# Gated cross-attention and top-2 expert block, 1 core: routed-row stores of the last two chunks placed one per expert tile

## What is computed

```python
x = x + tanh(g_xattn) * attention(layernorm(x), ctx, ctx)     # rotary q, k; 16 heads
n = layernorm(x)
xn = rms_norm(n) * norm_scale
scores = xn @ w_router.T                                     # 8 experts
ids = top_k(scores, 2); c = softmax(scores)[ids]
h = xn @ w_up[e].T; val, gate = split(h); h = val * silu(gate)
y = h @ w_down[e].T                                          # experts in ids only
x = x + tanh(g_ffn) * (sum(y * c) + n)
```

## Time and profile before

| | |
|---|---|
| median of 3 runs | 470.53 us (468.91 to 471.07) |
| the profiled execution | 470.41 us, of which 468.6 us is the span of the trace |
| PE busy | 411.8 us, 88% |
| DVE, ACT, POOL busy | 301.8, 261.7, 242.7 us |
| granted TensorE clock, mean | 0.917 of full |
| result stores (line 509) | 72, mean 1564 ns of POOL |
| row stores (line 427) | 64, mean 979 ns of POOL |

### The profile page before, as it was taken

How to read it: one execution, slowest core, us unless ns; L and a number is a source line. 1 busy time by engine, 2 the same in 40 slices (tenths; PEclk the granted TensorE clock), 3 DMA queues, 4 the chain that set the end, 5 groups by cost and what they waited for, 6 DMA issues and landing times.

```text
span 468.6 us, 13323 instructions
## 1 busy us (share of the span) xinstructions
PE 411.8 (88%) x3821; PEld 278.8 (59%) x3824; DVE 301.8 (64%) x1167; ACT 261.7 (56%) x582; POOL 242.7 (52%) x201
## 2 busy tenths in 40 slices
PE   7988899988898898989898939996799998999991
PEld 3445465645555466555555627674577876777871
DVE  6877888987878677777884414563655554555550
ACT  3437586977777676666665415752255554555540
POOL 6090242365446454454333475568466537886663
PEclk9998999999998897996956778998899999999997
DMA  7714341446579224232011322444334423344330
GB/s 185 177 47 126 75 112 35 121 135 173 145 206 232 63 65 115 77 88 79 30 43 48 87 52 43 68 59 94 59 48 61 58 47 49 56 57 56 37 28 0
DMA packets 57422, 39.07 MB, mean 83 GB/s; under 512 B 8819, under 2 KB 55158, under 8 KB 57366
## 3 DMA queue, kind: packets, MB, share of 16 engines
q1 hardware_dynamic: 43622, 28.87, 23.9%
q0 software_dynamic: 12736, 8.64, 13.1%
q10 hardware_dynamic: 1008, 0.85, 0.8%
HBM read 14.26 MB, written 11.75 MB: 56 GB/s over the span
## 4 chain that ended last, share of the span: by engine, by line
PE 61%; DVE 15%; issue 7%; ACT 5%; DMA 5%; another core or an unknown queue 4%; POOLq 1%; POOL 0%; DVEq 0%; ACTq 0%
PE bank L1595 9%; PE bank L1573 8%; PE bank L1575 7%; PE bank L1361 5%; DVE nmx L840 5%; PE bank L1585 4%; DMA out<-ys,yi 4%; PE bank L1388 3%; PE bank L1393 3%; PE bank L1335 3%; PE bank L1348 2%; PE bank L1303 2%; ACT pt L573 2%; PE bank L1304 2%
## 5 line engine op out<-in xcount | busy, mean ns | idle before, releaser
L509 POOL DMA_INDIRECT out<-ys,yi x72 | 112.6, 1564 | 63.8 <-issue 35.3
L427 POOL DMA_INDIRECT slots_dram<-xr,slu x64 | 62.7, 979 | 68.9 <-ACT pt L573 55.3
L840 DVE TENSOR_REDUCE nmx<-bank 128x4 f32<-128x512 f32 x128 | 81.8, 681 | 5.9 <-PE bank L1335 5.7
L1595 PEld LDWEIGHTS bank<-wf_sb,hT 128*128 128x128 f32 (+1 forms) x432 | 58.6, 197 | 39.0 <-issue 35.2
L1595 PE MATMUL bank<-wf_sb,hT 128*128 (+1 forms) x432 | 63.7, 285 | 19.9 <-DVE hT L1203 15.4
L573 ACT ACTIVATE pt<-bank 128x512 f32<-128x512 f32 x128 | 72.5, 594 | 14.6 <-PE bank L1348 12.8
L1193 DVE TENSOR_TENSOR hh<-sg,bank 128x352 f32<-128x352 f32 x72 | 37.5, 520 | 53.5 <-ACT sg L707 28.4
L715 ACT ACTIVATE ys<-bank,yc 128x128 f32<-128x128 f32 x72 | 26.5, 368 | 76.6 <-PE bank L1595 32.0
L1573 PE MATMUL bank<-wf_sb,xT 128*128 x144 | 58.1, 487 | 0.1
L1361 PE MATMUL bank<-pt,v 128*9 128x128 f32 x1024 | 53.7, 296 | 3.5 <-ACT pt L573 2.5
L1575 PE MATMUL bank<-wf_sb,xT 128*128 x144 | 55.9, 470 | 0.0
(11 more groups left out here) (191 smaller groups left out, 699.9 us busy)
## 6 DMA issues: line engine op xcount, KB each, us to landing
qs<-parts SPq DMA_DIRECT2D x48, 128.0 KB
ks<-parts SPq DMA_DIRECT2D x45, 128.0 KB
xs<-slots_dram SPq DMA_DIRECT2D x72, 66.0 KB
wf_sb<-in_wup SPq DMA_DIRECT2D x8, 352.0 KB
x_sb<-in_x SPq DMA_DIRECT2D x8, 256.0 KB, 3.5
ctx_sb<-in_ctx_in SPq DMA_DIRECT2D x8, 256.0 KB, 3.7
out<-x_sb SPq DMA_DIRECT2D x8, 256.0 KB, 2.4
out<-ys,yi POOLq DMA_INDIRECT x72
```

The lines of the kernel that those rows point to most:

```text
L427: nc.gpsimd.indirect_dma_start(out=slots_dram, out_offset=bass.IndirectOffsetOnAxis(ap=slu[:, c % 2, k, kk:kk + 1], axis=0), in_=xr[:, c % ...
L509: nc.gpsimd.indirect_dma_start(out=out.rearrange("b s d -> (b s) d"), out_offset=bass.IndirectOffsetOnAxis(ap=yi[:, r:r + 1], axis=0), in_ ...
L840: nc.vector.tensor_reduce(nmx[:, b % 2, at:at + 4], SB[g % 2][:, :].rearrange("p (h s) -> p h s", h=4), AX.X, ALU.max, negate=True).then_i ...
L1595: last = mm(Y[:, 0:D], hT[0:wide, r % 2, 128 * n:128 * n + 128], wf_sb[0:wide, bass.ds(w + 2 * H + n * D, D)], start=(n == 0), stop=(n == ...
```

## The change

The eight row stores of chunk 6 no longer run ahead of the tiles: one is issued ahead of each of the result stores 0 to 7. Those of chunk 7 are issued one ahead of each of the result stores 14 to 21, in place of two ahead of each of 14 to 17. Their number, their data and their order among themselves stay.

```diff
             scatter_both(NCH - 3, 3)
             power2(NCH - 1)
-            for k in range(CH):
-                scatter_both(NCH - 2, k)
 
             def send(q):
 
                 for r in range(R):
                     t = R * q + r
                     if isinstance(q, int):
-                        if 14 <= t < 14 + CH:
-                            scatter_both(NCH - 1, t - 14)
+                        if 0 <= t < 2 * CH:
+                            scatter(NCH - 2, t // 2, t % 2)
+                        if 14 <= t < 14 + 2 * CH:
+                            scatter(NCH - 1, (t - 14) // 2, t % 2)
```

## The result

The change is faster: 450.02 us median of four runs (447.54 to 451.32), against 470.43 us for the kernel before on the same chip (468.91 to 471.07, four runs). The ratio is 0.9576, with a 95% interval of 0.9532 to 0.9621.

What follows compares the result with a forecast made beforehand. PE was taken to set the pace, standing without work around row stores. 470.4 us, less 23.0 lost there, plus 12.5 for single row stores and 3.6 for half clock, gave 463.5 us; range 454 to 476.

Steps and rivals of the forecast that it cites:

- I take 0.78 us, from the single ones, since singles are what the change makes: 16 x 0.78 = 12.5 us.: Expert tiles: PE stands 0.78 us per single row store, the mean of five attention places; 12.5 us added.
- Together 23.0 us are lost around 16 row stores.: Tiles 0 to 4 lose 11.2 us and 15 to 19 lose 11.8, all of which the change can work on.
- Clock, 3.6 us.: Expert tiles after the change: two tiles at PE's half clock, 3.6 us added; bounds 0 and 10.8 us.
- POOL's floor, 454.3 us.: Tiles 0 to 21: if PE did not stand, POOL's queue would still cost 6.9 us in place of 23.0.
- More gain: Expert tiles: a single row store's stand is much shorter than in attention; down to 454.3 us; chance 0.15.
- No relief: Each row store costs PE 1.44 us wherever it stands; 470 us; chance 0.22, shared with another cause or clock.
- slower: Both groups of eight tiles: PE's stand goes on into the result store behind; 476 to 489 us; chance 0.20.
- Not due to row stores: Fetches of PE's code make it stand, at the same code places; 470 us; within the 0.22 for no change.
- store 0 near its tile's result: Sign at tile 0: its result store should start near 268 us, not 276.46.
- no step over 5: Sign in ACT's results, tiles 0 to 8 and 14 to 22: steps near 3.1 us each, none over 5.
- 1.28 and 1.9 us between POOL's instructions: Sign in POOL's list: 1.28 us from row store to result store, 1.92 from result store to next instruction.
- full clock as the sign that the clock term is too high: Sign in the tiles: full clock from tile 2 on would show the 3.6 us for half clock too high.

Runs made afterwards that it cites:

- the halves on chip 2: Kernel before (462.51 us) with only chunk 6's row stores one per tile: 452.09 us; with only chunk 7's one per tile: 456.94 us.
- the burst at tile 8: Kernel before with chunk 7 one per tile and chunk 6's eight row stores moved ahead of result store 8: 456.81 us, ratio 0.9854.

## Why the prediction was wrong

Its direction and its mechanism were right where it was made: PE stands in runs of row stores, and spreading them takes the stand away. It failed in these steps.

**"I take 0.78 us, from the single ones, since singles are what the change makes: 16 x 0.78 = 12.5 us."** This is the main error. With the plain stretches of chip 4 (9.61 us for tiles 0 to 4, 14.23 for 4 to 9, 11.07 for 15 to 19, 7.77 for 19 to 22) the change loses 0.0, 16.15 - 14.23 = 1.9, 0.6 and 8.49 - 7.77 = 0.7 us: 3.2 us for 16 row stores, 0.2 each. In the halves on chip 2 it was less still, for tiles 0 to 8 of the first 283.89 - 263.52 = 20.37 us against 276.68 - 256.68 = 20.00 on chip 4, and 18.89 against 18.84 for tiles 15 to 22 of the second. The 0.78 came from a selection: I had taken the five places at which a stand could be read off. There are 21 readings at which a row store is issued near the transpose (started at most 1.1 us ahead of it or 0.3 behind); at nine of them DVE reads at 0.31 to 0.44 us, and the other twelve, of which I had used five, go from 0.49 to 1.82. One of the nine is in PE's, DVE's and POOL's timeline of before:

```profile
104.50 0.96 POOL L427 DMA_INDIRECT slots_dram<-xr,slu  x1 [1.47 <-ACT pt L573]
...
104.61 0.28 PE L1393 MATMUL bank<-con,nmx 128*16 128x128 f32 x1
104.92 0.28 DVE L847 CAST mTs<-bank 16x128 bf16<-16x128 f32 x1
```

The mean of the 21 is 0.76 us, 0.45 above the plain 0.31. And a late reading isn't lost PE time: it is the delay at one reader.

**"Together 23.0 us are lost around 16 row stores."** 2.4 of them are chunk 7's routing (9.61 + 11.07 - 8 x 2.29 = 2.4), which stays. The stand was 20.6 us, 1.3 per row store.

**Clock, 3.6 us.** It was 0. The half clock had come with the long stands and went with them, so its cost was in the 20.6.

**POOL's floor, 454.3 us.** It set the low end of the range and was wrong in two places. POOL needs 3.16 us for a tile with a row store, never 4.03: the wait for a landing runs under the row store. And PE's own time for tiles 0 to 22 isn't 22 x 2.29 = 50.4 us but 313.97 - 256.68 = 57.3, just what I had worked out for POOL. The floor was no floor: on chip 4, where nothing stands, the change with its 16 single row stores takes 315.96 - 258.62 = 57.34 us for these tiles, as the kernel before does.

**The sum again.** 470.4 - 20.6 + 3.2 = 453.0 us. The median is 450.0. Of the 22.9 us by which the two profiled spans differ, 17.4 are these terms, 3.3 lie ahead of tile 0, where the lists are the same, and 2.2 behind tile 22. Executions of one kernel on that chip differ by 2 to 4 us, and the profiled one of after is the fastest of its four, so part of the rest is spread; the other part I can't place. On chip 2 the halves left no such rest.

**The rivals.** *More gain* is what happened, beyond the end that I had given it: the stand of a single row store is much shorter between tiles. Its sign was there, steps of 2.29 to 2.73 us for tiles 1 to 4, where I expected 3.1. *No relief* and *slower* fell with tiles 0 to 4 at 9.62 us. *Not due to row stores* fell with the burst at tile 8. The step in common to all of them was never said: that the trace of one chip speaks for the program. On chips 3, 4 and 6 the base of the sum is 0, and the gain of the change, timed on 4 and 6, is at most about half a per cent (ratios 0.9948 and 0.9983; the first is just clear of one, 0.9914 to 0.9983, and no stand explains it).

**Told beforehand and seen:** store 0 near its tile's result (265.58), no step over 5, 1.28 and 1.9 us between POOL's instructions, full clock as the sign that the clock term is too high.

## What to carry to other kernels

Where GpSimd issues indirect row stores back to back and TensorE's signals come several us after its recorded work, put something between them. A result store in between and a wait of 1.6 to 1.8 us for the landing took the stand away equally well; the result stores cost nothing on two chips that don't show the stand, and the wait was not tried there. But keep the cover for what waits behind on GpSimd's list. When a cost is read from places where it shows, count the places where it doesn't as well; and take the plain time of a stretch from the same stretch, routing and all, not from its fastest tile.

## What the runs showed of the hardware

The same program takes 461 to 470 us on chips 1, 2 and 5 and 438 to 439 us on chips 3, 4 and 6. The stand, in the attention part too, is where the difference lies: plain tiles step 2.29 us on all of them, and behind tile 22, where no row store is left, the kernel before takes 468.6 - 345.52 = 123.1 us on chip 1 and 436.5 - 313.97 = 122.5 on chip 4. POOL's, PE's and DVE's timeline of the kernel before on chip 4, at the places of the earlier trace rows:

```profile
95.63 1.09 POOL L427 DMA_INDIRECT slots_dram<-xr,slu  x1 [1.68 <-ACT pt L573]
...
96.00 0.28 PE L1393 MATMUL bank<-con,nmx 128*16 128x128 f32 x1
96.32 0.28 DVE L847 CAST mTs<-bank 16x128 bf16<-16x128 f32 x1 [0.15 <-PE bank L1393]
...
166.32 0.28 PE L1393 MATMUL bank<-con,nmx 128*16 128x128 f32 x1
166.63 0.28 DVE L847 CAST mTs<-bank 16x128 bf16<-16x128 f32 x1
```

The reading that took 0.98 us on chip 1 takes 0.32 here, the one of 1.08 takes 0.31, and none of the 21 is over 0.42. Tile 0's result comes at 256.68 us here and at 267.59 on chip 1. That the 48 row stores of the attention part make this difference (11 us, 0.2 each) fits, but was not tested, and it is 7 us on chip 5 (263.75). TensorE is not the only engine that shows it. SyncE's issue of a tile load (line 362; count, then shortest, median and longest in ns), first of the kernel before on chip 1, then on chip 4:

```profile
L362 SPq DMA_DIRECT2D xs<-slots_dram x72: 3/337/732, 252.1 to 435.5; - x72
L362 SPq DMA_DIRECT2D xs<-slots_dram x72: 332/338/385, 242.3 to 403.4; - x72
```

In the burst of chip 1, at 268.27 and at 272.68 us, an issue takes 0.71 us. The longest is 0.60 to 0.73 us in all nine traces of chips 1, 2 and 5, and 0.39 in all eleven of chips 3, 4 and 6. So SyncE's slow instructions, which I had expected in the run of eight on a chip like chip 5, are there (0.72 us), and this one number tells the two kinds of chip apart. But it is as long with the change (0.71 us), so whether close row stores cause it is not shown. ACT's result instruction takes 0.37 us on every chip, also at the stands, and POOL's row stores in the burst 0.96 on chips 1 and 4 alike.

"PE stands" is an inference. What the trace shows is that its signals come late. The last matmuls ahead of DVE's copy below (line 1585) are recorded at 269.68 us, and PE's next new group at 279.41 waits for this copy:

```profile
278.44 0.42 DVE L1202 COPY hT<-bank 128x256 f32<-128x256 f32 x1 [8.53 <-remote]
```

Whether the matmuls themselves stood or only their signals were late, the records don't tell; the next tiles wait in either case.

What it is on those chips that holds TensorE while GpSimd issues row stores closely, whether the chip itself or what else uses it, stays open. Nor does a run show whether the recording of the trace has a part in it; shortest issues of 3 ns against 332 are no times of work. The runs speak against the rows' length (one execution on chip 5), POOL's lateness (result store 0 18.5 us behind on chip 2, with tiles 0 to 5 at 11.90 us) and PE's place in its code, no more.
